# Cross-attention and a two-expert feed-forward net on one core: layer norms moved to ScalarE, the gate taken from one dot product

## What is computed

```
def _layernorm(x, axis=-1, eps=1e-05):
    m = mean(x); v = var(x)
    return (x - m) / sqrt(v + eps)

q = layernorm(x) @ Wq.T ; k = ctx @ Wk.T ; v = ctx @ Wv.T      (16 heads of 64)
attn = softmax(where(mask, -max, q k.T * SCALE))
x = x + (attn v) @ Wo.T + bo
xf = layernorm(x)
top1 = argmax(softmax(xf @ gate_w.T))                           (2 experts)
out = x + expert_net[top1](xf) + b2 of both + shared_net(xf)
```

## Time and profile before

| | us |
|---|---|
| median of 3 runs | 2103.31 |
| lowest of 3 runs | 2103.16 |
| span of the profiled execution | 2104.4 |
| attention stage within it | 0 to about 622 |

### The profile page before, as it was taken

How to read it: one execution, slowest core, us unless ns; L and a number is a source line. 1 busy time by engine, 2 the same in 40 slices (tenths; PEclk the granted TensorE clock), 3 DMA queues, 4 the chain that set the end, 5 groups by cost and what they waited for, 6 DMA issues and landing times. The chain is left out here.

```text
span 2104.4 us, 32601 instructions
## 1 busy us (share of the span) xinstructions
PE 1920.3 (91%) x11964; PEld 1211.9 (58%) x11965; DVE 1010.5 (48%) x1795; ACT 803.3 (38%) x1442; POOL 523.2 (25%) x506
## 2 busy tenths in 40 slices
PE   8888887888779999999999999999998989889997
PEld 6343443433346666666666666566665656556664
DVE  6889999999974333333333334222222222222222
ACT  4632232222224344444444444334333334334333
POOL 1065665666640000010000000122211111121211
PEclk9989999999989999999999999999999999999999
DMA  9144444443456222322222350611111010111100
GB/s 323 44 134 136 147 124 126 148 131 121 124 184 215 84 71 71 100 90 90 70 86 83 110 220 31 240 39 35 42 41 32 26 32 29 32 42 32 39 28 14
DMA packets 123640, 198.20 MB, mean 94 GB/s; under 512 B 20208, under 2 KB 61680, under 8 KB 123120
## 3 DMA queue, kind: packets, MB, share of 16 engines
q1 hardware_dynamic: 115584, 171.01, 24.5%
q0 software_dynamic: 7920, 25.17, 3.7%
HBM read 137.95 MB, written 58.98 MB: 94 GB/s over the span
## 5 line engine op out<-in xcount | busy, mean ns | idle before, releaser
L999 DVE TENSOR_TENSOR room_a<-room_a 128x256 f16<-128x256 f32 (+1 forms) x528 | 233.6, 443 | 939.7 <-ACT room_a L986 939.6
L953 PE MATMUL pH<-room_a,room_f 128*128 128x256 f16 x4608 | 572.7, 275 | 34.9 <-issue 29.5
L965 PE MATMUL pY<-room_f,room_a 128*128 128x512 f16 x2304 | 559.6, 380 | 4.6 <-DVE room_a L999 4.6
L953 PEld LDWEIGHTS pH<-room_a,room_f 128*128 128x128 f16 x4608 | 454.8, 99 | 165.7 <-issue 39.7
L965 PEld LDWEIGHTS pY<-room_f,room_a 128*128 128x128 f16 x2304 | 225.6, 98 | 197.4 <-DVE room_a L999 4.9
L984 ACT ACTIVATE room_a<-pH,e_bsel,sc 128x256 f32<-128x256 f32 (+1 forms) x272 | 151.6, 557 | 457.6 <-PE pH L953 435.5
L984 ACT ACTIVATE room_a<-pH,b1s,sc 128x256 f32<-128x256 f32 x256 | 144.3, 564 | 374.8 <-PE pH L953 374.1
L456 PE MATMUL pO<-room_v,room_b 128*128 (+1 forms) x768 | 200.8, 426 | 77.8 <-DVE room_b L660 77.8
L953 PE MATMUL pH<-room_a,room_v 128*128 128x256 f16 (+1 forms) x1728 | 204.5, 271 | 16.4 <-issue 16.1
L953 PEld LDWEIGHTS pH<-room_a,room_v 128*128 128x128 f16 x1728 | 163.8, 99 | 67.0 <-issue 20.7
L965 PE MATMUL pY<-room_v,room_a 128*128 128x512 f16 x816 | 198.1, 379 | 0.0
(11 more groups left out here) (187 smaller groups left out, 1775.5 us busy)
## 6 DMA issues: line engine op xcount, KB each, us to landing
room_b<-in_w SPq DMA_DIRECT2D x64, 256.0 KB, 4.3
s_er<-in_w SPq DMA_DIRECT2D x32, 512.0 KB, 6.4
rows_room<-in_x SPq DMA_DIRECT2D x32, 256.0 KB, 4.7
room_a<-in_sw SPq DMA_DIRECT2D x32, 256.0 KB, 5.0
room_b<-in_x SPq DMA_DIRECT2D x32, 256.0 KB, 2.9
s_split<-room_a SPq DMA_DIRECT2D x64, 128.0 KB, 4.3
x_scratch<-room_b SPq DMA_DIRECT2D x32, 256.0 KB, 3.1
z_scratch<-room_b SPq DMA_DIRECT2D x32, 256.0 KB, 3.4
```

The lines of the kernel that those rows point to most:

```text
L953: mm = q.matmul(self.pH[j % 2][:, 0:rows], w[:, k, j * P:(j + 1) * P], zt[:, u, k, 0:rows], start=(n == 0), stop=(n == 3 * KC - 1))
L965: mm = q.matmul(self.pY[u][r][:, :], h[:, j % self.HR, r * P:(r + 1) * P], w[:, j, :], start=(j == 0 and n == 0), stop=(j == HC - 1 and n ...
L999: q.tensor_tensor(self.hl[:, j % self.HR, 0:rows], self.hf[:, j % self.HR, 0:rows], self.hh[:, j % self.HR, 0:rows], ALU.subtract).then_in ...
```

## The change

Both norms are now written as activations with a scale and a shift per row: x * rs + (-mean * rs). ScalarE computes them (`normal`, `normal2`) in its own queue; `exp` now stands ahead of `scale_w`. GpSimd makes the shift: `rstd` has four small instructions instead of two. The gate rows are subtracted once, before the loop; VectorE then takes one dot product of (x1 - mean) with that difference, and the choice (`pick`, moved behind `largest_w`) multiplies it by rs and compares it with the tie bound. In the front, the statistics of tile 0 are taken at split 15 of the second half instead of 23, its `rs` stands ahead of GpSimd's last partition reduction instead of behind it, and its normal is in ScalarE's queue. Small additions: a constant of -1, a wait in `stats` for the `rs` of two tiles earlier, and a wait in `rstd` for the normal of two tiles earlier.

The diff, cut to its core:

```diff
--- before.py
+++ after.py
@@ -516,6 +521,19 @@
                             at_least(e, S["att"], count(g, u) - 1)
                             e.activation(pTh[:, :, :], pP[:, :].rearrange("p (k n) -> p k n", k=PAIRS), ACT.Copy, scale=P_SCALE).then_inc(S["pTh"], 1)
 
+                        def normal(e, g, u):
+                            e.wait_ge(S["rs"], count(g, u))
+                            at_least(e, S["xT"], count(g, u) - 2)
+                            e.activation(xn[:, u % 2, :], xb[:, u, :], ACT.Identity, bias=shift1[:, u % 2, :],
+                                         scale=rs[:, u % 2, :]).then_inc(S["xn"], 1)
+
+                        def normal2(e, g, u):
+                            e.wait_ge(S["rs2"], count(g, u))
+                            if not isinstance(g, int) or N * g + u >= 2:
+                                e.wait_ge(S["z_out", u % 2], dma_count2(g, u) - 16)
+                            e.activation(z[:, u % 2, :], x1[:, u % 2, :], ACT.Identity, bias=shift2[:, u % 2, :],
+                                         scale=rs2[:, u % 2, :]).then_inc(S["z"], 1)
+
                         def scale_w(e, g, u):
 
                             s_col = (SW1, SW2)[u % 2]
@@ -547,6 +565,8 @@
                                 act.wait_ge(linked, LINKS_V)
                             if n >= NM and n % PAIRS == 0:
                                 act.wait_ge(w_seen, 10 + 2 * ((n - NM) // PAIRS + 1))
+                            if n == NF - 5:
+                                normal(act, 0, 0)
                             if n == NF - 1:
                                 hi_x(act, 0, 0)
                             act.wait_ge(f_done, n + 1)
@@ -556,11 +576,14 @@
                         def body(g):
                             for u in range(N):
                                 step(act, g, u, 0, hi_p)
+                                step(act, g, u, 1, exp)
                                 if not first_tile(g, u, 2):
                                     step(act, g, u, 2, scale_w)
-                                step(act, g, u, 1, exp)
+                                step(act, g, u, -1, normal2)
                                 if not first_tile(g, u, 3):
                                     step(act, g, u, 3, hi_x)
+                                if not first_tile(g, u, 4):
+                                    step(act, g, u, 4, normal)
                                 if first_tile(g, u, 2):
                                     step(act, g, u, 2, scale_w)
                                 if last_tile(g, u):
@@ -573,6 +596,7 @@
                     def _(pool):
                         pool.memset(kd, 0.0).then_inc(zeroed, 1)
                         pool.memset(vd, 0.0).then_inc(zeroed, 1)
+                        pool.memset(minus[:, :], -1.0)
                         pool.memset(half[:, :], -0.5).then_inc(S["half_set"], 1)
                         pool.memset(eps[:, :], EPS).then_inc(S["half_set"], 1)
                         pool.memset(ident[:, :], 0.0).then_inc(made, 1)
@@ -590,17 +614,20 @@
                         pool.partition_all_reduce(amr[:, 0:2], am[:, 0:2], P, RMAX).then_inc(reduced, 1)
                         pool.wait_ge(amaxed, 4)
                         pool.partition_all_reduce(amr[:, 2:4], am[:, 2:4], P, RMAX).then_inc(reduced, 1)
-                        pool.wait_ge(s_max, 3)
-                        pool.partition_all_reduce(amsr[:, :], ams[:, :], P, RMAX).then_inc(reduced, 1)
                         pool.wait_ge(S["half_set"], 2)
 
-                        def rstd(src_sem, mv, ve, rs, ves, done):
+                        def rstd(src_sem, mv, ve, minus_m, rs, shift, ves, made_rs, used, done):
+
                             def fn(e, g, u):
 
                                 e.wait_ge(src_sem, count(g, u))
-                                e.tensor_tensor(ve[:, u % 2, :], mv[:, u % 2, 1:2], eps[:, :], ALU.add).then_inc(ves, 1)
+                                e.tensor_tensor(ve[:, u % 2, :], mv[:, u % 2, 1:2], eps[:, :], ALU.add)
+                                e.tensor_tensor(minus_m[:, u % 2, :], mv[:, u % 2, 0:1], minus[:, :], ALU.mult).then_inc(ves, 1)
                                 e.wait_ge(ves, count(g, u))
-                                e.tensor_tensor(rs[:, u % 2, :], ve[:, u % 2, :], half[:, :], ALU.pow).then_inc(done, 1)
+                                at_least(e, used, count(g, u) - 2)
+                                e.tensor_tensor(rs[:, u % 2, :], ve[:, u % 2, :], half[:, :], ALU.pow).then_inc(made_rs, 1)
+                                e.wait_ge(made_rs, count(g, u))
+                                e.tensor_tensor(shift[:, u % 2, :], minus_m[:, u % 2, :], rs[:, u % 2, :], ALU.mult).then_inc(done, 1)
                             return fn
 
                         def sub(e, g, u):
@@ -630,10 +657,12 @@
                             e.wait_ge(S["sws"], count(g, u))
                             e.tensor_tensor(swl[:, u % 2, :], sw[:, u % 2, :], swh[:, u % 2, :], ALU.subtract).then_inc(S["swl"], 1)
 
-                        rs_1 = rstd(S["agg"], mv, ve, rs, S["ve"], S["rs"])
-                        rs_2 = rstd(S["agg2"], mv2, ve2, rs2, S["ve2"], S["rs2"])
+                        rs_1 = rstd(S["agg"], mv, ve, mm1, rs, shift1, S["ve"], S["rs_x"], S["xn"], S["rs"])
+                        rs_2 = rstd(S["agg2"], mv2, ve2, mm2, rs2, shift2, S["ve2"], S["rs_z"], S["z"], S["rs2"])
 
                         rs_1(pool, 0, 0)
+                        pool.wait_ge(s_max, 3)
+                        pool.partition_all_reduce(amsr[:, :], ams[:, :], P, RMAX).then_inc(reduced, 1)
                         pool.memset(least, -NEG).then_inc(S["half_set"], 1)
                         lo_x(pool, 0, 0)
                         pool.wait_ge(S["const_in"], 48)
@@ -662,6 +691,7 @@
 
                         def stats(e, g, u):
                             e.wait_ge(S["x_in", u], dma_count(g))
+                            at_least(e, S["rs"], count(g, u) - 2)
                             e.bn_stats(st[:, u % 2, :], xb[:, u, :]).then_inc(S["stats"], 1)
 
                         def stats_done(e, g, u):
@@ -693,11 +723,6 @@
                             e.wait_ge(S["x1"], count(g, u))
                             e.bn_stats(st2[:, u % 2, :], x1[:, u % 2, :]).then_inc(S["stats2"], 1)
 
-                        def normal(e, g, u):
-                            e.wait_ge(S["rs"], count(g, u))
-                            at_least(e, S["xT"], count(g, u) - 2)
-                            e.tensor_scalar(xn[:, u % 2, :], xb[:, u, :], mv[:, u % 2, 0:1], rs[:, u % 2, :], ALU.subtract, ALU.mult).then_inc(S["xn"], 1)
-
                         def dropped(e, g, u):
 
                             e.wait_ge(S["m_in", u], dma_count(g))
@@ -726,17 +751,18 @@
                             e.tensor_tensor(amw[:, 0:2], amw[:, 0:2], ewm[:, u % 2, :], ALU.max).then_inc(S["amw"], 1)
 
                         def gate(e, g, u):
+                            e.scalar_tensor_tensor(out=junk[:, :], in0=x1[:, u % 2, :], scalar=mv2[:, u % 2, 0:1], in1=gw[:, 1, :],
+                                                   op0=ALU.subtract, op1=ALU.mult, accum_out=gg[:, u % 2, :]).then_inc(S["gd"], 1)
+
+                        def pick(e, g, u):
+                            e.wait_ge(S["gd"], count(g, u))
                             e.wait_ge(S["rs2"], count(g, u))
-                            e.tensor_scalar(z[:, u % 2, :], x1[:, u % 2, :], mv2[:, u % 2, 0:1], rs2[:, u % 2, :], ALU.subtract, ALU.mult).then_inc(S["z"], 1)
-                            e.wait_ge(S["z"], count(g, u))
-                            for k in range(2):
-                                if k == 1:
-                                    e.wait_ge(S["g0"], count(g, u))
-                                e.tensor_tensor_reduce(junk[:, :], z[:, u % 2, :], gw[:, k, :], 1.0, 0.0, ALU.mult, ALU.add, gg[:, u % 2, k:k + 1]).then_inc(S[f"g{k}"], 1)
-                            e.wait_ge(S["g1"], count(g, u))
-
-                            e.tensor_scalar(expert1[:, bass.ds(N * g + u, 1)], gg[:, u % 2, 1:2], gg[:, u % 2, 0:1], TIE,
-                                            ALU.subtract, ALU.is_gt).then_inc(S["pick1"], 1)
+
+                            e.tensor_scalar(expert1[:, bass.ds(N * g + u, 1)], gg[:, u % 2, :], rs2[:, u % 2, :], TIE,
+                                            ALU.mult, ALU.is_gt).then_inc(S["pick1"], 1)
+
+                        def agg2_done(e, g, u):
+                            e.wait_ge(S["agg2"], count(g, u))
 
                         def largest(dst, t, done, arrived=None):
                             if arrived is not None:
@@ -811,12 +837,10 @@
                                 dve.wait_ge(w_seen, 19)
                                 for c, (a0, a1) in enumerate(((SEEN_S1, SEEN_S2), (SEEN_S2, SEEN_B1), (SEEN_B1, SEEN_B1 + 1))):
```

(22 more changed lines are left out.)

## The result

The changed kernel takes 1997.07 us (median of 4 runs, 1995.23 to 1997.15), the kernel before 2103.23 on the same chip: ratio 0.9498, 95% interval 0.9484 to 0.9512. One of the four runs of the kernel before took 2854.9 us; it is left out of the ratio, and nothing recorded says why it was slow. The forecast was 2002. Of this, the attention stage has 105.6: the first shared-net matmuls start at 517.59 instead of 623.17 us.

What follows compares the result with a forecast made beforehand. VectorE was taken to bound the attention stage. Savings of 92.3 us in the loop, 5.8 in front and 3 in the tail, together 101.1, came off the 2104.4 us span, less 1.1 to the median: 2002 us, range 1982 to 2042.

Steps and rivals of the forecast that it cites:

- The bound before: Attention loop, first stage: VectorE is the engine without slack and sets the round of 15.95 us.
- VectorE's additions: VectorE per round: dot product 0.75 us, accumulator read and pick 0.3; waits for GpSimd raise its need from 9.96 to 13.1.
- rival E: ScalarE: a table switch around each new function, two or three a round, about 2045 us; chance 0.02.
- rival C: Small instructions and the port cost twice the estimate: GpSimd over 13 us, VectorE at 14, 2046 us; chance 0.1.
- The floor: TensorE in the attention loop: unchanged work, attention matmuls at least 11.67 us apart.
- The clock: TensorE in the loop: shorter rounds remove the long wait, granted clock 1.00, matmuls near 5.35 us, 1.6 us less in those rounds.
- rival B: Attention matmuls stay at half clock because waits remain scattered, rounds of 13.3 to 13.6 us, 2029 us; chance 0.15.
- The round after: Attention loop: 12.4 us, the middle of 11.67 and 13.1; 3.55 us saved in each of 26 rounds, 92.3.
- D: Loop: normal2's wait for rs2 closes a ring of 23.9 us; once per round it gives 2300 us, slower; chance 0.02.
- rival A: TensorE alone sets the round as the dot product wins the port race: 11.7 us a round, 1984 us; chance 0.2.
- The front: Before the loop: first score matmuls near 105.3 us, 6.4 saved less 0.6 for the gate rows: 5.8, bounds 0 and 8.
- The tail: Tiles 28 to 31, the first non-floor round and the last pick together: 3 us saved, bounds 0 and 6.

Runs made afterwards that it cites:

- e5: Kernel before with the gate rows subtracted once and one dot product instead of two, norms still on VectorE: 2037.47 us, ratio 0.9684.
- e9: e3 without the running maximum on VectorE; each tile's maxima get own columns, reduced once behind the loop: 1978.51 us, ratio 0.9412.
- e10: Changed kernel with hi_x ahead of normal2 on ScalarE: 2000.53 us, ratio 0.9515.
- e11: The changed kernel itself, run again as the mark for differences below 1%: 2001.66 us, ratio 0.9514.
- e6: Kernel before with only the front changed (statistics of tile 0 at split 15, rs ahead of the last partition reduction): 2098.75 us, ratio 0.998.
- e3: Changed kernel with add_bo ahead of the rs chains on GpSimd and the dot product behind largest_w on VectorE: 1986.09 us, ratio 0.9447.

## Why the prediction was right

The measured 1997.07 us lies in the range of 1982 to 2042.

*The bound before* (VectorE, without slack): right. 7.04 us taken from it shortened the round, and e5 shows that a single product comes off whole.

*VectorE's additions.* The dot product free of GpSimd was put at 0.75 and is 0.74; behind `norm` at 2.5 and is 2.48; it does both. The Trainium skill's rule ("SBUF — State Buffer", section "Who interferes with whom"), which no row of before showed for this form, agrees with the trace: 742 to 2486 ns. `largest_w`'s maximum was to wait up to 1.4 us more and takes this long (VectorE's groups, 200 to 500 us):

```profile
L751 DVE TENSOR_TENSOR amw<-amw,room_b 128x2 f32<-128x2 f32 x24 | 20.1, 836 | 0.8
```

*ScalarE.* 0.72 to 1.0 us per norm; measured:

```profile
L534 ACT ACTIVATE room_b<-room_b,shift,rs 128x512 f32<-128x512 f32 x25 | 20.3, 813 | 88.2 <-POOL shift L630 88.2
...
L527 ACT ACTIVATE room_a<-rows_room,shift,rs 128x512 f32<-128x512 f32 x22 | 17.8, 810 | 0.0
```

There is one table load in the trace of after, too, 1283 ns at the start: rival E is out. (What the prediction cites of the Trainium skill, "ScalarE: Activation LUTs", on cheap functions stands in that page's section "Table sets: the hidden batching unit", not in the one named.)

*GpSimd.* The small instructions were put at 0.86 us a round; from the start of the first (340.04) to the start of `norm` (342.48) it is now 2.44, and the same stretch, from the first addition to L614, was 388.28 - 386.71 = 1.57: 0.87, so rival C is out. One of each pair:

```profile
L630 POOL TENSOR_TENSOR shift<-mm,rs 128x1 f32<-128x1 f32 x47 | 11.7, 248 | 3.7
...
L625 POOL TENSOR_TENSOR mm<-mv,minus 128x1 f32<-128x1 f32 x47 | 9.4, 199 | 0.0
```

*The floor* of 11.67 us: exact, as e9 shows in 26 rounds. *The clock*: right, 1.00 in the loop; rival B is out.

*The round after.* The 12.4 was the middle between TensorE's floor and VectorE's worst need, and the round is 12.45, but this step was right in size only, and that the middle met the round is luck. What sets the round is neither bound alone: it is the ring of residual, `rs`, `norm`, `lo_x` and `add_bo`, with VectorE's queue level with it where the dot product loses. The prediction named the members but looked for a ring in the new wait of `normal2` (D). That one has room: e10 takes `hi_x` out of it and the time stays. It did not look for the one-round ring that was there. It also gave rival A the wrong effect: VectorE winning the race was to bring the floor of 11.67; in e11 it won in all but one of 22 rounds between 200 and 480 us, and the round was 12.52.

*The front* was put at 5.8 us: the score matmuls started 5.9 earlier, of which e6 keeps 4 to the end. *The tail* was put at 3: tiles 28 to 31 take 506.94 - 476.54 = 30.4 instead of 36.2 us, and tiles 0 to 2 lost their wait as well (23.3 instead of 24.6); and between the first score matmuls and tile 0 another 1.6 us went (23.7 instead of 25.3). The term should have been 8.7 (5.8, the 2.8 us by which tile 2 gained more than the score matmuls, and 0.1 at the end); it is the one that was mis-sized. With 90.9 for 92.3 in the loop it makes the 4.5 us between the 101.1 forecast and the 105.6 measured.

## What to carry to other kernels

When the busiest engine of a pipelined loop is relieved, the next bound can be no engine but a ring of dependences that closes once per round; walk from one instruction to its next copy along what released each, and sum. An instruction with early inputs (here `add_bo`) that stands late in a queue puts itself on such a ring for nothing: move it to where its engine waits. Keep tiny two-input VectorE instructions away from a busy GpSimd; a 2-element maximum of 0.16 us took up to 1.7 here, and e3 without it is 7.6 us shorter.

## What was not expected

The winner of a race for GpSimd's port gained nothing by it. A VectorE product of 0.74 us that went first made GpSimd's `norm` take 2.39 to 2.46 instead of 1.90 us, and since `norm` was on the ring, the round came out 0.12 us longer than the same round with the race lost. In the rows above the two starts lie 0.03 to 0.12 us apart, and the same kernel falls out differently from one execution to the next: 10 of 22 races won in the profiled execution at 12.45 us a round, 21 of 22 in e11 at 12.52.

The partition reduction (L594), recorded at 0.37 us, was followed in the kernel before by nothing on GpSimd until 104.07 (L601), 8 us after its start at 95.95. In the changed kernel it starts at 97.11, a memset (L666) is recorded at 97.38, and then `lo_x` comes at 104.51, 7.4 us after the reduction's start and 0.65 after ScalarE's `hi_x` had ended. This suggests that the reduction holds GpSimd far longer than its record says; no run here isolates it.
